# Second layer: offset products between the third query group's, positions in fewer steps, three convolution taps from VectorE to TensorE

## The reference

```
x_ln = layernorm(x)
q = x_ln @ wq + bq
o = gelu(depthwise_conv7x7(q, stride 2) + dw_b)        # 16 x 16 positions
offsets = conv1x1(o)                                   # 2 numbers for each of the 256 positions
deformed = refs + tanh(offsets)
grid = (deformed + 1) * (h / 2) / 2, then (grid + 1) * 0.5 * (w - 1), clipped to the image
interp = four gathered corners of x, weighted by the fractions   # 256 rows
k = v = interp @ wv + bv
out = attention(q @ mq_w, k @ mk_w, v @ mv_w) @ mo_w + x, then a layer norm, an mlp, gelu and the sum
```

## Time and profile before

| | |
|---|---|
| median of three runs | 4038.05 us (4036.7 to 4046.57) |
| the profiled execution: its own time | 4036.7 us |
| the profiled execution: span from first to last instruction | 4035.0 us |
| mean granted clock of TensorE | 0.987 |
| busy: TensorE, VectorE, ScalarE, GpSimd | 3865.6, 2966.9, 2507.4, 1638.9 us |

### The profile page before, as it was taken

How to read it: one execution, slowest core, us unless ns; L and a number is a source line. 1 busy time by engine, 2 the same in 40 slices (tenths; PEclk the granted TensorE clock), 3 DMA queues, 4 the chain that set the end, 5 groups by cost and what they waited for, 6 DMA issues and landing times. The chain is left out here.

```text
span 4035.0 us, 63980 instructions
## 1 busy us (share of the span) xinstructions
PE 3865.6 (96%) x22126; PEld 3260.5 (81%) x22126; DVE 2966.9 (74%) x5158; ACT 2507.4 (62%) x5497; POOL 1638.9 (41%) x1935
## 2 busy tenths in 40 slices
PE   8999999999999999999999988999999999999999
PEld 6888888888888888878878856777777777777777
DVE  3984984975966957938849737878787878787876
ACT  3883864865846847838838615656565656565656
POOL 1332432422432432323324305555555555555554
PEclk9999999999999999999999989999999999999999
DMA  2221221221221221222212132222222222222221
GB/s 86 43 64 45 50 64 42 44 79 36 64 63 27 59 63 32 54 63 43 64 42 50 55 110 61 79 70 77 71 78 70 79 70 78 70 77 70 77 74 58
DMA packets 117736, 252.28 MB, mean 63 GB/s; under 512 B 17772, under 2 KB 34216, under 8 KB 117416
## 3 DMA queue, kind: packets, MB, share of 16 engines
q1 hardware_dynamic: 112808, 231.41, 21.3%
q0 software_dynamic: 4608, 16.78, 1.3%
HBM read 97.12 MB, written 33.55 MB: 32 GB/s over the span
## 5 line engine op out<-in xcount | busy, mean ns | idle before, releaser
L626 DVE TENSOR_REDUCE a_neg_max<-a_ps 128x1 f32<-128x1024 f32 x512 | 625.0, 1222 | 336.7 <-PE a_ps L449 336.7
L725 POOL TENSOR_TENSOR a_qk<-a_fold_s,a_fold_r 64x256 f32<-64x256 f32 x256 | 191.4, 748 | 1228.8 <-DVE a_fold_s L634 1228.8
L584 ACT ACTIVATE a_ph<-a_ps 128x512 fp32r<-128x512 f32 x1024 | 556.9, 593 | 171.3 <-PE a_ps L463 168.3
L643 DVE TENSOR_TENSOR a_pl<-a_ps,a_ph 128x512 fp32r<-128x512 f32 x1024 | 654.7, 680 | 8.9 <-ACT a_ph L584 5.7
L591 ACT ACTIVATE a_prob<-a_ps,a_neg_max 128x1024 f32<-128x1024 f32 x512 | 572.3, 1118 | 17.6 <-DVE a_neg_max L626 11.8
L463 PEld LDWEIGHTS a_ps<-a_ident,a_prob 128*128 128x128 f32 x4096 | 469.8, 140 | 112.6 <-issue 46.8
L463 PE MATMUL a_ps<-a_ident,a_prob 128*128 128x128 f32 x4096 | 540.7, 274 | 17.3 <-DVE a_pl L643 16.2
L484 PE MATMUL a_ps<-a_ph,a_v 128*128 128x256 f32 x2048 | 550.7, 302 | 0.0
L484 PE MATMUL a_ps<-a_pl,a_v 128*128 128x256 f32 x2048 | 509.2, 282 | 0.0
L448 PE MATMUL a_ps<-a_kh,a_qs 128*128 128x512 f32 x1024 | 408.3, 399 | 12.0 <-POOL a_kl L716 12.0
L449 PE MATMUL a_ps<-a_kl,a_qs 128*128 128x512 f32 x1024 | 404.8, 395 | 0.0
(11 more groups left out here) (265 smaller groups left out, 9316.0 us busy)
## 6 DMA issues: line engine op xcount, KB each, us to landing
a_qs<-a_qk SPq DMA_DIRECT2D x128, 256.0 KB, 3.7
a_kl<-a_qk SPq DMA_DIRECT2D x128, 256.0 KB, 4.4
a_xtok<-in_x SPq DMA_DIRECT2D x64, 256.0 KB, 4.6
b_xs<-x SPq DMA_DIRECT2D x64, 256.0 KB, 4.6
b_qs<-b_qh SPq DMA_DIRECT2D x64, 256.0 KB, 3.3
b_qs<-b_ql SPq DMA_DIRECT2D x64, 256.0 KB, 3.8
b_z<-x SPq DMA_DIRECT2D x64, 256.0 KB, 3.7
out<-b_ot SPq DMA_DIRECT2D x64, 256.0 KB, 2.0
```

What stands on the lines that cost most here:

```text
L584: act.activation(ph[:, b % 2, 4 * g:4 * g + 4, (u % 2) * P:(u % 2 + 1) * P], ps[:, 4 + n % 2, :].rearrange("p (k q) -> p k q", k=4), ACT.C ...
L626: dve.tensor_reduce(neg_max[:, i_:i_ + 1], ps[:, 2 * (i_ % 2):2 * (i_ % 2) + 2, :] .rearrange("p a b -> p (a b)"), AX, ALU.max, negate=Tru ...
L643: dve.tensor_tensor(pl[here], ps[:, 4 + n % 2, :].rearrange("p (k q) -> p k q", k=4), raw(ph[here]), ALU.subtract).then_inc(pl_ok, 1)
```

## The change

Four edits, all in layer 1. `DVE_TAPS` goes from 29, 23, 22, 22 to 29, 22, 21, 21, so that TensorE does 17 taps in place of 16 for tiles 1, 2 and 3. The third query group no longer stands behind tile 3's taps but behind the wait for `taps_upto[1]`, its bank is 6 in place of 0, and after each three of its products come two offset products, now with one bank for each half of the positions. The positions are reached in four steps in place of seven ahead of the indices, with constants that the setup prepares (`ref`, `ref_low`); the exact position is made behind the indices. The arithmetic gives the same positions.

```diff
--- before.py
+++ after.py
@@ -35,6 +35,7 @@
 SB_START = 16512
 SB_END = 229344
 WHOLE = float(2 ** 23)
+HALF_EDGE = 0.5 * (HW - 1)
 
 
 class Region:
@@ -788,7 +789,7 @@
 
     PAIRS = ((0, 1), (2, 3))
     POOL_TAPS = [10, 10, 11, 11]
-    DVE_TAPS = [29, 23, 22, 22]
+    DVE_TAPS = [29, 22, 21, 21]
     PRODUCTS = 6
     SOLO = 20
     PE_SUM, POOL_SUM = -1, -2
@@ -824,6 +825,8 @@
         bmlp = R.take("b_bmlp", [P, C])
         refs = R.take("b_refs", [P, 2, NS])
         ref = R.take("b_ref", [P, 2, KT])
+        ref_low = R.take("b_ref_low", [P, 2, KT])
+        turned = R.take("b_turned", [P, 2, KT])
         pos = R.take("b_pos", [P, 2, KT])
         low_at = R.take("b_low_at", [P, 2, KT])
         row_at = R.take("b_row_at", [P, KT])
@@ -1146,6 +1149,12 @@
                 dve.wait_ge(pe_s, 23)
                 dve.tensor_copy(ref[:], ps[:, 4, :].rearrange("p (c s n) -> p c s n", c=2, s=KT)[:, :, :, 0])\
                    .then_inc(chn, 1)
+                dve.wait_ge(chn, 9)
+                dve.tensor_scalar(ref[:], ref[:], 1.0, HW / 2 / 2.0, ALU.add, ALU.mult).then_inc(chn, 1)
+                dve.wait_ge(chn, 10)
+                dve.tensor_scalar(ref[:], ref[:], 1.0, HALF_EDGE, ALU.add, ALU.mult).then_inc(chn, 1)
+                dve.wait_ge(chn, 11)
+                dve.tensor_scalar(ref_low[:], ref[:], 0.5, None, ALU.subtract).then_inc(chn, 1)
                 dve.wait_ge(pe_s, 24)
                 dve.tensor_tensor(bmo[:], ps[:, 2, :], bo_raw[:], ALU.add).then_inc(chn, 1)
                 dve.tensor_tensor(bmlp[:], ps[:, 3, :], bm_raw[:], ALU.add).then_inc(chn, 1)
@@ -1158,9 +1167,9 @@
 
         nc.all_engine_barrier()
 
-        QUERY_BEHIND = (0, 2, 3)
-        QH_BANK = (4, 5, 0, 7, 2, 3, 4, 5)
-        OFF_BANK = 1
+        QUERY_BEHIND = (0, 2)
+        QH_BANK = (4, 5, 6, 7, 2, 3, 4, 5)
+        OFF_BANK = (0, 1)
         K_BANK = (6, 7, 2, 3)
         V_BANK = (6, 7)
         MO_BANK = (0, 1, 6)
@@ -1184,7 +1193,7 @@
         EACH.update({s.num: 192 for s in s_ld})
         EACH.update({s.num: 64 for s in o_st})
         EACH.update({dg_ok.num: len(pe_taps), dg_used.num: len(pe_taps), tap.num: len(taps), ptap.num: sum(pool_ops), prod_ok.num: len(act_taps), off_ps.num: 1,
-                     tanh_ok.num: 1, pos_ok.num: 7, near_ok.num: 4, it_ok.num: 4 * KT})
+                     tanh_ok.num: 1, pos_ok.num: 5, near_ok.num: 4, it_ok.num: 4 * KT})
         steps = [0]
 
         def window(c, n):
@@ -1273,13 +1282,23 @@
                     pe.wait_ge(y_ok, at(y_ok, c - 1))
                 projection(1, c)
 
+            def offsets(k):
+
+                pe.wait_ge(gelu_ok, at(gelu_ok, k + 1))
+                for st in range(KT):
+                    mm = pe.matmul(ps[:, OFF_BANK[st], 0:2], o[:, k, st * P:(st + 1) * P],
+                                   vec[:, 20:28].rearrange("p (c k) -> p c k", c=2)[:, :, k],
+                                   start=k == 0, stop=k == CT - 1)
+                if k == CT - 1:
+                    mm.then_inc(off_ps, 1)
+
             def queries(groups):
 
                 for g in groups:
                     if g < 2:
                         pe.wait_ge(q_sb, at(q_sb, CT + g + 1))
                     if g == 2:
-                        pe.wait_ge(tap, at(tap, taps_upto[0]))
+                        pe.wait_ge(tap, at(tap, taps_upto[1]))
                     if g >= 6:
                         pe.wait_ge(qh_sb, at(qh_sb, g - 5))
                         pe.wait_ge(ql_sb, at(ql_sb, g - 5))
@@ -1288,7 +1307,10 @@
                     for k in range(CT):
                         mm = three(pe, ps[:, QH_BANK[g], :], (wh["wqm"][:, k, n], wl["wqm"][:, k, n]),
                                    (xh[s][:, k, :], xl[s][:, k, :]), k == 0, k == CT - 1)
-                    mm.then_inc(qh_ps, 1)
+                        if k == CT - 1:
+                            mm.then_inc(qh_ps, 1)
+                        if g == 2:
+                            offsets(k)
 
             for e, (c, n) in enumerate(pe_taps):
                 first, last = n == first_pe[c], n == KS * KS - 1
@@ -1300,16 +1322,7 @@
                 if last and c in QUERY_BEHIND:
                     queries((QUERY_BEHIND.index(c),))
 
-            pe.wait_ge(tap, at(tap, taps_upto[1]))
-            for st in range(KT):
-                for k in range(CT):
-                    if st == 0:
-                        pe.wait_ge(gelu_ok, at(gelu_ok, k + 1))
-                    mm = pe.matmul(ps[:, OFF_BANK, 2 * st:2 * st + 2], o[:, k, st * P:(st + 1) * P],
-                                   vec[:, 20:28].rearrange("p (c k) -> p c k", c=2)[:, :, k],
-                                   start=k == 0, stop=k == CT - 1)
-            mm.then_inc(off_ps, 1)
-            queries(range(3, 8))
+            queries(range(2, 8))
 
             for st in range(KT):
                 pe.wait_ge(ih_ok, at(ih_ok, st + 1))
@@ -1497,7 +1510,7 @@
             act.wait_ge(tap, at(tap, len(taps)))
             query(0)
             act.wait_ge(off_ps, at(off_ps, 1))
-            act.activation(pos[:], ps[:, OFF_BANK, 0:2 * KT].rearrange("p (s c) -> p c s", c=2), ACT.Tanh)\
+            act.activation(turned[:], ps[:, 0:2, 0:2].rearrange("p s c -> p c s"), ACT.Tanh)\
                .then_inc(tanh_ok, 1)
             query(1)
             query(2)
@@ -1653,24 +1666,21 @@
             query(0)
 
             dve.wait_ge(tanh_ok, at(tanh_ok, 1))
-            dve.tensor_tensor(pos[:], pos[:], ref[:], ALU.add).then_inc(pos_ok, 1)
+            reach = HW / 2 / 2.0 * HALF_EDGE
+            dve.scalar_tensor_tensor(low_at[:], turned[:], reach, ref_low[:], ALU.mult, ALU.add).then_inc(pos_ok, 1)
             dve.wait_ge(pos_ok, at(pos_ok, 1))
-            dve.tensor_scalar(pos[:], pos[:], 1.0, HW / 2 / 2.0, ALU.add, ALU.mult).then_inc(pos_ok, 1)
+            dve.tensor_scalar(low_at[:], low_at[:], WHOLE, WHOLE, ALU.add, ALU.max).then_inc(pos_ok, 1)
             dve.wait_ge(pos_ok, at(pos_ok, 2))
-            dve.tensor_scalar(pos[:], pos[:], 1.0, 0.5 * (HW - 1), ALU.add, ALU.mult).then_inc(pos_ok, 1)
+            dve.tensor_scalar(low_at[:], low_at[:], WHOLE + HW - 2, WHOLE, ALU.min, ALU.subtract).then_inc(pos_ok, 1)
             dve.wait_ge(pos_ok, at(pos_ok, 3))
-            dve.tensor_scalar(low_at[:], pos[:], 0.5, 0.0, ALU.subtract, ALU.max).then_inc(pos_ok, 1)
-            dve.wait_ge(pos_ok, at(pos_ok, 4))
-            dve.tensor_scalar(low_at[:], low_at[:], HW - 2.0, WHOLE, ALU.min, ALU.add).then_inc(pos_ok, 1)
-            dve.wait_ge(pos_ok, at(pos_ok, 5))
-            dve.tensor_scalar(low_at[:], low_at[:], WHOLE, None, ALU.subtract).then_inc(pos_ok, 1)
-            dve.wait_ge(pos_ok, at(pos_ok, 6))
             dve.scalar_tensor_tensor(row_at[:], low_at[:, 0, :], float(HW), low_at[:, 1, :], ALU.mult, ALU.add)\
                .then_inc(pos_ok, 1)
-            dve.wait_ge(pos_ok, at(pos_ok, 7))
+            dve.wait_ge(pos_ok, at(pos_ok, 4))
             for y in range(2):
                 dve.tensor_scalar(idx[:, y, :], row_at[:], float(TOK * r + HW * y), None, ALU.add).then_inc(idx_ok, 1)
+            dve.scalar_tensor_tensor(pos[:], turned[:], reach, ref[:], ALU.mult, ALU.add).then_inc(pos_ok, 1)
             query(1)
+            dve.wait_ge(pos_ok, at(pos_ok, 5))
             dve.tensor_tensor(near[:, 0], pos[:], low_at[:], ALU.subtract).then_inc(near_ok, 1)
             dve.wait_ge(near_ok, at(near_ok, 1))
             dve.tensor_scalar(near[:, 1], near[:, 0], 1.0, None, ALU.subtract).then_inc(near_ok, 1)
```

## The result

| | median | lowest to highest |
|---|---|---|
| before (4 runs) | 4041.98 us | 4036.7 to 4046.57 us |
| after (4 runs) | 4074.56 us | 4071.01 to 4078.09 us |

The ratio is 1.0074, with an interval of 1.0061 to 1.0087: the change makes the kernel 30 us slower (0.0074 x 4042). The forecast was 4046.5 us, and its range of 4033 to 4059 us doesn't hold the time.

A forecast was written before the change was run, and what follows sets the result against it. VectorE's tail was taken to set when the offset products start, then TensorE's own work; +2.3 us without falls plus +6.2 us for two falls made +8.5 us on 4038.05 us: 4046.5 us, range 4033 to 4059 us.

The forecast's parts named there:

- VectorE's tail: End of layer 1's convolution: with three taps moved, VectorE waits 1.4 us on TensorE and ends 0.2 us later.
- the gap and the third group: Behind TensorE's taps: it idles 1.85 us, then the third query group's 12 products lie on the path, 2.83 us an image.
- the offset products: Between the third group's products: the 16 spread instructions still cost 2.3 us an image, as before.
- The sum without falls: All eight images of layer 1 together, if the clock never falls: +2.3 us.
- Rival (a): Offset products: clock cured and loads hidden under neighbouring streams, 2.3 us more saved an image, -16.1 us, 4022 us; chance 0.10.
- the clock term: Stretch behind TensorE's taps: two images fall to half clock at 3.1 us each (bounds 1.6 and 4.7), +6.2 us.
- my own signs of being wrong: A third group with offsets under 4 us, a tail ending at 3084 us, or falls in none or all images.
- rival (b): Four or more clock falls; six give +20.9 us, 4059 us; far end, eight falls, 4065 us; chance 0.27.
- the positions cost nothing: Ahead of the gathers: three steps fewer, gathers 1.6 us later, covered by VectorE's queue; without cover up to 1.6 us an image.

The follow-up runs named there:

- e3: The changed kernel with eight throw-away products of 512 columns in TensorE's gap ahead of the third query group; 4043.74 us, ratio 1.0009.
- e8: The changed kernel with its 16 offset products in one piece behind the third query group, the gap left; 4053.33 us, ratio 1.0024.
- e4: The kernel before, third query group left as filler, offset products spread between the fourth group's products, banks renumbered; 4077.06 us, ratio 1.0092.
- e5: The kernel before with three taps moved to TensorE and the shorter positions, third group and offset products where they stood; 4019.84 us, ratio 0.9943.
- e7: As e5, but with one tap moved to TensorE in place of three (29, 22, 22, 22); 4017.89 us, ratio 0.9942.
- e6: The kernel before with the shorter positions alone; 4036.79 us, ratio 0.9979.
- e2: The kernel before with the three taps moved to TensorE alone; 4033.75 us, ratio 0.9986.
- e1: The changed kernel with only its tap numbers undone, three taps back on VectorE; 4075.95 us, ratio 1.0083.
- e9: e4 with SyncE waiting for the four gathers before it copies the queries; 4076.22 us, ratio 1.0076.
- e10: e7 with the query copies held back until the gathers have landed, as in e9; 4034.14 us, ratio 0.9975.

## Why the prediction was wrong

The table sets the eight images' distances from tap to score side by side with layer 1 as a whole. "On the path" is the sum of tap to K and K to score over eight images, less the 251.2 us of the kernel before, and plus 1.45 us an image where three taps moved (0.48 us where one did); layer 1 is span less start, less 1604.3 us.

| kernel | half clock behind the taps | tap to K, us | on the path | layer 1 | ratio |
|---|---|---|---|---|---|
| before | 6.8 us in six | 22.8 x6, 20.4, 19.7 | 0 | 0 | 1 |
| after | 10.1 us in six, 6.8 in two | 25.32 x6, 23.76 x2 | +31.5 | +35.0 | 1.0074 |
| e3, gap filled | none | 20.58 x7, 21.03 | -0.4 | +4.7 | 1.0009 |
| e8, not spread | 3.4 us in five | 22.15 x5, 20.59 x3 | +6.2 | +14.9 | 1.0024 |
| e4, fourth group | none there, around K in eight | 22.5 to 23.7 | +30.3 | +35.5 | 1.0092 |
| e5, third stays | none | 18.48 x8 | -19.6 | -19.5 | 0.9943 |
| e7, one tap | none | 18.41 x8 | -26.3 | -22.6 | 0.9942 |

"On the path" and "layer 1" differ mainly by short falls further on: from about the first score product on the trace shows half clock for 3.4 us three times in the changed kernel, five times in e3, seven in e8, once in e5 and four times in e7, and never in the kernel before (leaving out the last ten us of each run).

**Right: VectorE's tail.** Forecast: it waits 1.4 us on TensorE's taps and ends 0.2 us later. Measured: 1.31 us in the changed kernel, 1.40 in e5; from the start of the long run of taps to the end of the sums it was 16.57 us (3084.91 - 3068.34) and is 16.81 us (3102.92 + 1.09 - 3087.20).

**Right: the gap and the third group.** TensorE idles 1.92 us (1.85 said) and the third group lies on the path.

**Nearly right: the offset products.** I took 2.3 us, from rows in which they still waited for the GELUs: I took off the 0.16 us that the row gives as idle, and the waits between them were longer. Without one, 16 take 1.76 us in e5 (3082.33 - 3080.57) and 1.70 us in e8 (3098.98 - 3097.28). At the full clock K's first product stands 20.58 us behind the taps, 21.1 said; the whole difference is this term. The sum without falls was +2.3 us, and e3 has -0.4 us of it on the path. Rival (a), loads hidden under the neighbours, is out: in e3 the stretch from the third group to K is 3107.95 - 3089.29 = 18.66 us, of which 72 products of 0.236 us are 16.99 and 1.67 us are left for the 16 spread ones, as much as in one piece.

The Trainium skill (TensorE: Matmul & The Clock Gate, section "LDWEIGHTS (loading the stationary operand)") gives the load of 128 columns as 128 / 1.2 ns = 0.107 us. At the full clock the trace agrees, with 0.106 and 0.110 us for each offset product (1.70 and 1.76 us over 16), which fits loads in a row that set their pace. At half clock it doesn't: four offset products take 0.70 us up to the next product in the changed kernel (3105.69 - 3104.99), and 0.36 us in e3 (3090.45 - 3090.09).

**The step that failed: the clock term.** The prediction says "I take two, a fall at 3.1 us (bounds: 1.6 us where it is half as long, 4.7 us where it lasts half as long again, because the thin stretch goes on under it): +6.2 us". Both factors were too small. The number: falls came in all eight images, not in two, which was one of my own signs of being wrong; what happened is rival (b), past its far end. The size: against e3's 20.58 us a fall costs 25.32 - 20.58 = 4.74 us in six images and 23.76 - 20.58 = 3.18 us in two, together 34.8 us, where six falls at 3.1 us were there before. The three prices seen (1.56 us in e8, 3.18 and 4.74 us here) go with 3.4, 6.8 and 10.1 us at half clock, just under half of each. The bound of 4.7 us was right, and I should have given it to rival (b) with its own reason: under the fall the kernel goes on with exactly the stretch that was thin. With eight falls at that price the sum would have been 2.3 + 37.6 = +39.9 us; with what was measured it is 2.3 + 34.8 = +37.1 us, for the +35.0 us of layer 1. About 2.5 us come back behind K, where the first scores wait less: K to score is 71.6 us over eight images, and 74.1 us in e3. Of the 35.0, +31.5 us stand in the rows between tap and score; the other 3.5 us are about what the three short falls cost that the trace shows some 45 us behind the taps in images 1, 5 and 6: image 5, with one of them, took 206.6 us from tap to tap, and images 3, 4 and 7, as long at half clock behind the taps but without one, 205.2 to 205.3 us.

The reason for "two" was that the images would no longer come at equal distances, so where an image stands in time would decide. They came at 205.0 to 206.6 us, so the order was broken, and yet every image fell; what differed was when the fall began and how long it lasted. That the stretch in front had grown from 0.44 to 1.92 us of idling was the stronger argument, and I had it. The Trainium skill (the same page, section "What's actually happening") has half rate as the default that activity lifts; e3 agrees, as with eight products in the gap the clock stayed up.

**The two halves of the cause.** The gap is needed: with it filled (e3) the clock falls in no image behind the taps, though the products are spread. In e4, with 0.15 to 0.30 us of idling, it stays up too until TensorE idles ahead of K. The spreading is needed for the size: with the gap alone (e8) the loss is a third. Together they give the 0.74%.

**Wrong, and small: the positions cost nothing.** I hid them behind VectorE's queue. Alone (e6) they give 0.9979, and e5 stands at 0.9943 against 0.9986 for e2, in another set of runs. Part of it is seen: e2's 4.3 us of waits for gathered rows at two lines become 0.2 us, and K to score, 76.7 us over eight images, becomes 72.1 us. The cover was full in the kernel before, where six images had their queries at half clock, and thin in e2, where seven had them at full clock; that the one comes from the other fits, but no run separates it. The rest is not settled: in e6 the images fall in another pattern than before (three images for 6.8 us and two for 3.4 us), so its gain holds clock as well as work.

**Open.** Why a fall that began later was shorter, why one of eight images kept its clock in e1 and three in e8, and what starts the short falls in the score stage. In e9 one sum took VectorE 6.26 us, and the same sum took 2.5 us once in e1 (image 3) and once in e6 (image 1), where the gaps were longer too; why is not known. It is in e9's 1.0076.

## What to carry to other kernels

Work that fills a wait on TensorE is worth more than its own time: it keeps the clock up for what comes behind it, so price a gap as the gap plus the fall that may follow it, just under half of the time at half clock: 1.6 to 4.7 us an image here, most where the stretch behind mixes short products in. Cure a falling clock by closing the gap in front, not by spreading the short products behind it: with one or three taps moved and the shorter positions (e7 and e5) the kernel is 0.57 to 0.58% faster, with the three taps alone (e2) 0.14%. And before moving the step that issues gathers, look at which bulk copies its transfers will meet: with 3.2 us of head start for 7.7 us the gathers took half as long again, and the kernel (e4) lost as much as the changed one. The collision is not all of that loss, since e9 took it away and the time stayed.

## What the runs showed of the hardware

- A gap of 1.92 us, in which the record of the clock still reads 1.00, was followed by half clock in all eight images, within 1.7 us of the restart in six and later in two (the changed kernel). With the short products in one piece (e8) five of eight images fell; with 8 products in the gap (e3), none in the 18 us behind the taps.
- In six of eight images the clock fell behind 0.28 and 0.16 us of idling at 16 short products (before). In the 30 images of e2, e5, e7 and e10 without such idling it fell behind the taps in none, in the two with it (e2, e10) in both.
- Time at half clock cost just under half of itself: 1.56, 3.18 and 4.74 us for 3.4, 6.8 and 10.1 us.
- Four products of two columns, each with a load of 128, took 0.36 us at the full clock and 0.70 us at half clock up to the next product.
- An indirect gather took 9.8 us in the median with the query copies 3.2 us behind the first of four, and 6.1 us with the copies held back.
